# A graph network layer: every third eviction of the node transform moves from ScalarE to VectorE, and a clearing moves from VectorE to GpSimd

## The reference, cut to what matters

```python
h = maximum(layernorm(x), 0)                 # 12500 nodes x 128
# linear transform of the nodes, times the node's attribute a
l1 = [h_s @ lin1_ws, h_v @ lin1_wv] * a / sqrt(32)
# 200000 edges, sorted by dst: gather l1[src], weight it by a small network of the distance,
# multiply with the edge attributes, and sum by dst
msg = f(l1[src], edge_attr, mlp(rbf(distance)))
agg = segment_sum(msg, dst) / clip(count, 1)
# second transform, gate and skip branch
l2 = agg @ lin2 * a / 8;  alpha = tanh(agg @ alpha_w * a / 8)
out = x + (h @ sc) * a / sqrt(32) + alpha * l2
```

## Time and profile before

| what | value |
|---|---|
| time, median of 3 runs | 2078.52 us (2077.29 to 2079.92) |
| the profiled execution | 2077.13 us |
| its span | 2075.2 us |
| GpSimd busy | 1517.7 us (73%) |
| TensorE busy | 1791.7 us (86%) |
| VectorE busy | 1660.9 us (80%) |
| ScalarE busy | 1121.9 us (54%) |

### The profile page before, as it was taken

One profiled execution on the slowest core, in us unless ns is written; L12 is line 12 of the kernel. 1 busy time (PEld: TensorE's weight loads), 2 busy tenths in 40 slices (PEclk: granted clock), 3 DMA queues, 4 the chain that ended last, 5 costly groups with the idle time before them and its releaser, 6 DMA issues. The chain is left out here.

```text
span 2075.2 us, 42789 instructions
## 1 busy us (share of the span) xinstructions
PE 1791.7 (86%) x9991; PEld 1217.4 (59%) x9991; DVE 1660.9 (80%) x4500; ACT 1121.9 (54%) x3242; POOL 1517.7 (73%) x1619
## 2 busy tenths in 40 slices
PE   6599989988998898889888888898988898889883
PEld 6466666666665666556556555565655555556552
DVE  8688888878888888878777877877787878788877
ACT  6565655555555656544444555454545544555545
POOL 5577777777777777777777777777777777777770
PEclk9799999999999989999899989989998999998996
DMA  7433232323223232222222222222222222222224
GB/s 220 110 70 66 64 69 66 69 64 68 66 63 68 66 70 63 60 56 60 58 59 56 59 59 57 58 59 58 57 59 59 58 58 59 59 58 58 59 59 131
DMA packets 334451, 142.05 MB, mean 68 GB/s; under 512 B 249827, under 2 KB 308892, under 8 KB 334428
## 3 DMA queue, kind: packets, MB, share of 16 engines
q0 software_dynamic: 50016, 102.51, 18.9%
q1 hardware_dynamic: 284412, 39.28, 11.6%
HBM read 127.87 MB, written 13.75 MB: 68 GB/s over the span
## 5 line engine op out<-in xcount | busy, mean ns | idle before, releaser
L795 POOL DMA_INDIRECT lin_g<-lin_table,src_ix x1563 | 1482.3, 948 | 486.7 <-issue 476.0
L965 ACT ACTIVATE lin_sh<-lin_g,meta 128x128 f32<-128x128 f32 x1563 | 484.4, 389 | 197.6 <-DMA lin_g<-lin_table,src_ix 196.9
L840 PE MATMUL ps_w<-w,h 128*128 128x256 f32 x1566 | 488.9, 457 | 5.9 <-DVE msg L1169 3.3
L852 PE MATMUL ps_near<-msg,onehot 128*64 128x257 f32 x3126 | 423.3, 407 | 0.0
L1138 DVE TENSOR_TENSOR lin_sh<-lin_g,ps_meta 128x576 f32<-128x576 f32 (+1 forms) x261 | 196.4, 753 | 278.1 <-DMA lin_g<-lin_table,src_ix 277.4
L840 PEld LDWEIGHTS ps_w<-w,h 128*128 128x128 f32 x1566 | 374.1, 272 | 51.0 <-ACT h L954 11.4
L864 PE MATMUL ps_sums<-far_hot,near_sums 128*128 128x128 f32 x1044 | 203.8, 323 | 204.8 <-DVE agg L1196 204.1
L864 PEld LDWEIGHTS ps_sums<-far_hot,near_sums 128*128 128x128 f32 x1044 | 153.2, 211 | 366.0 <-issue 365.1
L852 PEld LDWEIGHTS ps_near<-msg,onehot 128*64 128x64 f32 x3126 | 213.2, 145 | 180.8 <-issue 110.2
L820 PE MATMUL ps_h<-rbf,w 32*128 32x192 f32 x1044 | 240.0, 349 | 18.6 <-DVE rbf L1125 18.0
L947 ACT ACTIVATE h<-ps_h 128x384 f32<-128x384 f32 x261 | 127.8, 490 | 214.4 <-PE ps_h L820 214.1
(11 more groups left out here) (150 smaller groups left out, 1905.4 us busy)
## 6 DMA issues: line engine op xcount, KB each, us to landing
lin_g<-lin_table,src_ix POOLq DMA_INDIRECT x1563
dist_in<-in_edge_weight SPq DMA_DIRECT2D x67, 96.0 KB
xq<-in_x SPq DMA_DIRECT2D x24, 256.0 KB, 3.6
lin_table<-lin_out SPq DMA_DIRECT2D x24, 256.0 KB, 3.0
x_in<-in_x SPq DMA_DIRECT2D x24, 256.0 KB
out_dram<-skip SPq DMA_DIRECT2D x24, 256.0 KB
src_ix<-in_src SPq DMA_DIRECT2D x268, 3.0 KB, 4.4
meta<-in_edge_attr SPq DMA_DIRECT2D x264, 12.0 KB
```

The source lines that it names most:

```text
L795: pool.indirect_dma_start(lin_g[rows, u, t, :], None, lin_table, bass.IndirectOffsetOnAxis(ap=src_ix[rows, u, col:col + 1], axis=0)).then_ ...
L840: mm = pe.matmul(ps_w[:, 2 * j * P:(2 * j + 2) * P], cols[:, j, :], w3[:], start=True, stop=True)
L852: mm = pe.matmul(ps_near[half * NEAR:(half + 1) * NEAR, 0:MSG + 1], onehot[:, u % 2, t, :], msg[:, u % 2, t, :], start=(j == 0), stop=(j = ...
L965: last = act.activation(lin_sh0[:, u % 2, j, :], lin_g[:, u, j, :], ACT.Copy, scale=meta[:, u, harm_col(j):harm_col(j) + 1])
```

## The change

Steps n with n % 3 == 2 (2, 5, ..., 23, eight of them) are evicted by VectorE, with one `tensor_tensor` of the 128x512 values in `psN` with `row_scale` spread over the columns (`evict`). It counts on a semaphore of its own, `evicted_dve`, and `wait_evicted` makes the stores and `product(n + 2)` wait for the right one of the two. In VectorE's order `evict(n - 3)` stands behind `means(n)` and `scale`, and ahead of the constants and the windows. `evict(23)` stands behind the last `scale`, ahead of `places`. ScalarE leaves these steps out. VectorE's memset of `agg` is taken away, and GpSimd clears that quarter behind `normalize(24)`, its last, with one memset.

```diff
+            def by_dve(n):
+                return n % 3 == 2 and 0 <= n < STEPS
+            def wait_evicted(eng, n):
+                if n >= 0:
+                    mine = sum(by_dve(k) for k in range(n + 1))
+                    eng.wait_ge(evicted_dve if by_dve(n) else evacuated, mine if by_dve(n) else n + 1 - mine)
...
                     def store(n):
-                        sp.wait_ge(evacuated, n + 1)
+                        wait_evicted(sp, n)
...
                     for n in range(STEPS + 1):
                         normalize(n)
                         if 4 <= n < 4 + PIECES:
                             lo, hi = CLEAR_POOL * (n - 4) // PIECES, CLEAR_POOL * (n - 3) // PIECES
                             pool.memset(agg[:, lo:hi], 0.0).then_inc(agg_zero, 1)
+                    pool.memset(agg[:, CLEAR_POOL:], 0.0).then_inc(agg_zero, 1)
...
                         copy_hT(n + 1)
-                        evacuate(n)
+                        if not by_dve(n):
+                            evacuate(n)
...
                         pe.wait_ge(hT_ready, n + 1)
-                        at_least(pe, evacuated, n - 1)
+                        wait_evicted(pe, n - 2)
...
+                    def evict(n):
+                        dve.wait_ge(lin_done, n + 1)
+                        dve.wait_ge(scale_set, n // 2 + 1)
+                        at_least(dve, lin_stored[n % OB], 16 * (n // OB))
+                        scaling = row_scale[:, n * NB:(n + 1) * NB].unsqueeze(2).to_broadcast([P, NB, DIM])
+                        dve.tensor_tensor(lin_out[:, n % OB], psN[:, n % 2], scaling, ALU.mult).then_inc(evicted_dve, 1)
...
                     for w in (w_lin1, w_sc_m, w1, w2, w_lin2, w3):
                         dve.memset(w[:], 0.0).then_inc(weights_zeroed, 1)
-                    dve.memset(agg[:, CLEAR_POOL:], 0.0).then_inc(agg_zero, 1)
                     stats(0)
...
                         means(n)
                         if n % 2 == 0:
                             scale(n // 2 - 1)
+                        if by_dve(n - 3):
+                            evict(n - 3)
                         if n == 8:
...
                     factor(PAIRS_1 - 1)
                     scale(PAIRS_1 - 1)
+                    for n in range(STEPS - 2, STEPS):
+                        if by_dve(n):
+                            evict(n)
                     places()
```

More of the change, by code:

```diff
@@ L217, in gnn_kernel @@
             mean_kept = sem("mean_kept")
+            evicted_dve = sem("evicted_dve")
             agg_zero, windows_set = sem("agg_zero"), sem("windows_set")
```

## The result

Measured over 20 runs each: 2081.0 us (2078.7 to 2083.23) against 2077.51 us before. The ratio is 1.0016, 95% interval 1.0010 to 1.0022: slower by 3.3 us (2.1 to 4.6). Forecast was +4.5 us, 2083.0 us, with a range of 2077.5 to 2087.5. The medians differ by 3.5 us; +3.3 us is the ratio times the median before.

A forecast was written before the change was run, and what follows sets the result against it. GpSimd's gathers run without pause, so the time of the first gather sets the whole. 0 (start) + 1.0 + 0.6 + 2.5 + 0 + 0.4 (tail) = +4.5 us, 2083.0 us; range 2077.5 to 2087.5.

The forecast's parts named there:

- Start: VectorE's start without the memset: gain hidden by waits for step 6's x and the first store; 0, bounds 0 to 2.3 us gain.
- Clearing on GpSimd: Memset behind GpSimd's last subtraction: 3.2 us, covered by some 7 us without other GpSimd work; cost 0, bounds 0 and 3.2.
- Price of one eviction: One 128x512 tensor_tensor on VectorE with one input in PSUM: 0.69 us, bounds 0.35 and 1.15.
- Step 5: VectorE's eviction at n = 8: wait 1.7 us plus 0.62, less 1.34 of idle; +1.0 us where windows(0) starts.
- Step 8: VectorE's eviction at n = 11, behind windows(0): product long done, so only the work, +0.62 us.
- Step 11: VectorE's eviction at n = 14: wait 1.85 us for a 2.08 us product, plus 0.62; +2.5 us.
- the rival of the higher clock: Each product takes 1.16 us, waits 0.9 in place of 1.9 us; about +2 us, 2080.5 us; chance 0.30.
- Sum to pair 7: Steps 5, 8 and 11 summed where windows(2) starts: +4.1 us; root of pair 7 at 45.8 instead of 41.65 us.
- Pair 7 to pair 12: Steps 14, 17, 20: ScalarE's 3.4 us relief is spent on waits; 0 net, bounds 3.4 gain and 1.5 loss.
- Tail: End of the front: evict(23) delays places; the edge stage starts at 73.65 instead of 69.15 us, +0.4 on the sum.
- The relief wins: VectorE meets finished products, ScalarE saves 4.6 us: 2074 us, chance 0.06; half-way case 2078, chance 0.07.
- The ring of output buffers: Two engines share three output buffers; one extra wait of 1 to 3 us for a store, 2085.5 us; chance 0.07.

The follow-up runs named there:

- the clearing alone: Kernel before with only the memset of agg's quarter moved from VectorE's start to GpSimd behind its last subtraction; two timings, ratios 1.0012 and 0.9997.
- The evictions alone: Changed kernel's eight evictions on VectorE, with the clearing left at VectorE's start; 2083.45 us against 2078.27 of the kernel before, ratio 1.0028.
- the early half: Changed kernel with only steps 2, 5, 8 and 11 evicted by VectorE, clearing moved; two timings, ratios 1.0015 and 1.0013 to the kernel before.
- the later evictions: Changed kernel with evict(n-4) in place of evict(n-3) behind means(n), same work on each engine; ratio 0.9996 to the kernel before.
- the work alone: Kernel before plus a VectorE memset of 740 scratch elements at the eight eviction places, without waits; ratio 1.0003, +0.6 us.
- the waits alone: Kernel before, ScalarE evicting everything, plus VectorE waits for the products at the eight eviction places; ratio 1.0012, +2.5 us.

## Why the prediction was right, by its steps

- **Sum and side.** +4.5 us forecast, +3.3 (2.1 to 4.6) measured. The fronts of the two pairs of profiles differ by 4.3 and 3.65 us. 0.16% lies inside the 0.2% that the forecast set as the edge, where it expected +0.22%; the chances were 0.49 and 0.45, and this case can't choose between them. That less than 0.2% can't be told from no change was too careful: with 20 runs each, the interval of 0.10 to 0.22% excludes no change.
- **Start, 0.** In the changed kernel right: 16.80 for 16.60 and 19.24 for 19.00. In the clearing alone it won 0.5 to 1.4 us, within the bound of 2.3. If the clearing is worth the 1.3 us of its fronts, the evictions cost 5.3 us on top of it, and the forecast's 0 and +4.5 would each be off by about 1 us and cancel, which would be luck. The evictions alone, with 2.5 us of front in one profile, don't bear that out, so it stays open.
- **Clearing on GpSimd, 0.** Right. 2.78 us instead of 3.2, as one long memset is cheaper by the element than the pieces of 603, and it ends at 66.94, 0.6 us ahead of `places`. A collision with L512's followers isn't seen.
- **Price of one eviction, 0.69 us.** 0.687.
- **Step 5, +1.0.** 1.7 us where `windows(0)` starts (27.42 for 25.75), as the product took 2.07 us, not 1.59. In the other profile it took 1.22, and the root of pair 7 came 0.9 us earlier.
- **Step 8, +0.6.** From `windows(0)` to `windows(1)` the delay grows by 0.5 us. Right.
- **Step 11, +2.5.** Wait 1.73 and 1.76 (1.85 forecast; the forecast's own rows give 37.95 - 36.14 = 1.81, and +2.4). Where the product had all or most of the full clock, in the evictions alone and the second profile of the early half, (products of 1.16 and 1.34 us), it was 0.84 and 1.03. This is the rival of the higher clock: both cases occur, in different executions, and the gap between the forecast and the median is of their size.
- **Sum to pair 7, +4.1.** 3.66 and 2.05 against each execution's partner before. Where `windows(2)` starts, which is where the forecast has its +4.1, it is 4.4 and 2.8. The term that was missing behind it is L466, 1.47 us before and 0.94 now, -0.5.
- **Pair 7 to pair 12, 0.** 19.58 and 19.27 us against 19.15 and 18.17: +0.8. Steps 14, 17 and 20 waited 2.85, 1.29 and 1.18 us (2.4, 1.5, 1.2 forecast). ScalarE's relief bought nothing, as forecast. But the reason given, that its 3.4 us are spent on the waits, isn't the whole one: with the waits gone (the later evictions) it bought nothing either.
- **Tail, +0.4.** From the root of pair 12 to the first gather 9.16 and 9.15 us, against 8.96 and 8.65. VectorE's last instruction at 72.43 (72.7), its first in the edge stage at 73.44 (73.65).
- **The relief wins.** Not here: it needed VectorE to meet finished products. With one iteration more it does (2.4 us of waits), and the loss is gone; that was shown by the later evictions. The rival's gain of 4.6 us is not there even then.
- **The other rivals and signs.** The memset didn't hold `places`. The ring of output buffers gave one wait, 3.46 us on ScalarE at 19.24, which ends as before; a store of the kernel before landed 2.3 to 4.2 us after its issue, not 2.7 to 4. VectorE's waits at the new line sum to 11.7 and 10.3 us (about 9 forecast), and the first gather came at 74.05 and 72.85 us (74.2 forecast).

## What to carry to other kernels

When an engine that is ahead of a pipeline takes over work from its end, count the wait for its input, and all that stands in order behind it, before the work. Here the work alone moved the median by +0.6 us (-1.2 to +2.5), the waits alone by +2.5 (0.6 to 4.4), and both together by +3.3. Place such a job where its input has surely come, here one iteration later, which took 9.3 of 11.7 us of VectorE's waits away for one of 1.1 us on TensorE. Then look for slack next to each wait: a wait shorter than an idle time that is there already is free. And work taken off an engine isn't a gain by itself: ScalarE's relief bought nothing here, with the waits or without.

## What the runs showed of the hardware that was not expected

A scalar_tensor_tensor of 8x768 on VectorE with both inputs in SBUF took 1.47 to 1.48 us where it started beside GpSimd's subtraction, and 0.93 to 0.94 us where it started behind the subtraction's end (L466 and its like, in all profiles). The Trainium skill (SBUF — State Buffer, Who interferes with whom) has this: two SBUF inputs contend with a GpSimd instruction that reads SBUF. The trace agrees, with 1.47 against 0.94 us. A memset of GpSimd beside it, from 37.73 to 38.33 us in the profile of the work alone, left it at 0.93 us. A change of order can thus give or take half a microsecond without touching the instruction.

The gathers took 1956.2 to 1958.4 us from first to last in seven executions with a granted clock of 0.91 to 0.92 over the span and 1961.1 us in one, the kernel with the evictions alone, whose median is late by more than its front. No edit lies there, and the cause wasn't found.
